# First cross attention of a decoder: scores from split q and k in one float32r pass, and five small operations on other engines

## What is computed

```
q = (x @ Wq + bq)                 # 16 heads of 8 channels
k = concat(fside @ Wk + bk, ctx)  # 248 keys: ctx itself serves as memory_k and memory_v
v = concat(fside @ Wv + bv, ctx)
attn = softmax((q @ k.T) * 8 ** -0.5, over keys)     # for each head
x = layernorm(x + (attn @ v) @ Wp + bp)
```

## Time and profile before

| | |
|---|---|
| median of 3 runs | 2702.93 us (2698.47 to 2707.09) |
| span of the profiled execution | 2695.8 us (its own time is not listed apart from the runs) |
| mean granted TensorE clock | 0.967 |
| TensorE busy, of the whole span | 2502.7 us (93%) |
| VectorE, ScalarE, GpSimd busy | 1849.6, 1737.7, 1401.1 us |
| DMA | 151.37 MB, mean 56 GB/s |

### The profile page before, as it was taken

The page is one execution under the profiler, slowest core; times in us unless marked ns, Lnnn a source line. Parts: engine busy times, 40 slices in busy tenths (PEclk is TensorE's granted clock), DMA queues, the critical chain, the costliest instruction groups (busy, mean ns, idle before and its releaser), DMA issues. The chain is left out here.

```text
span 2695.8 us, 95989 instructions
## 1 busy us (share of the span) xinstructions
PE 2502.7 (93%) x29950; PEld 2007.2 (74%) x29951; DVE 1849.6 (69%) x5434; ACT 1737.7 (64%) x6375; POOL 1401.1 (52%) x2914
## 2 busy tenths in 40 slices
PE   7999999799999999788889969999999799999995
PEld 6888888577777777487667758888888688888883
DVE  4565555588888888564334448888887388888886
ACT  4666666355555555213556638888888588888883
POOL 2333333233444344165774447777776266666664
PEclk9999999799999999899999979999999899999997
DMA  6332322211111111123332211111111111111100
GB/s 158 100 88 79 89 81 65 65 49 48 49 48 48 48 47 44 37 85 84 78 80 66 66 48 53 47 53 49 50 53 37 33 31 32 31 31 31 31 26 11
DMA packets 270161, 151.37 MB, mean 56 GB/s; under 512 B 51776, under 2 KB 263744, under 8 KB 270016
## 3 DMA queue, kind: packets, MB, share of 16 engines
q1 hardware_dynamic: 261312, 131.57, 18.2%
q0 software_dynamic: 8704, 17.97, 1.9%
HBM read 92.52 MB, written 48.51 MB: 52 GB/s over the span
## 5 line engine op out<-in xcount | busy, mean ns | idle before, releaser
L1187 ACT ACTIVATE pr<-psS,small 128x128 f32<-128x128 f32 x1024 | 366.7, 384 | 95.9 <-DVE small L1258 94.0
L1625 DVE TENSOR_REDUCE small<-psS 128x2 f32<-128x496 f32 x512 | 321.4, 669 | 90.3 <-PE psS L1489 89.1
L1577 ACT ACTIVATE pr<-psT 120x512 f32<-120x512 f32 (+1 forms) x384 | 215.1, 595 | 136.9 <-PE psT L1485 124.5
L1473 PE MATMUL psT<-cross_Qm,cross_xf 32*120 32x512 f32 (+1 forms) x768 | 292.1, 641 | 0.5 <-ACT pr L1577 0.2
L1187 ACT ACTIVATION_READ_ACCUMULATOR pr<-psS,small 128x1 f32 x1024 | 226.1, 221 | 0.0
L1478 PE MATMUL psS<-cross_xf,cross_Qm 32*128 32x248 f32 x1024 | 209.1, 428 | 1.1 <-DVE small L1625 1.1
L2172 POOL DMA_INDIRECT results<-experts_ob,experts_xb x144 | 138.5, 962 | 115.4 <-ACT experts_ob L1992 100.5
L1258 DVE TENSOR_REDUCE small<-psS 128x8 f32<-128x1024 f32 x128 | 156.7, 1224 | 60.5 <-PE psS L1152 60.3
L2112 DVE SCALAR_TENSOR_TENSOR experts_bgh<-experts_bth,psS 128x256 f32<-128x256 f32 x144 | 60.7, 421 | 198.9 <-ACT experts_bth L1984 198.9
L956 POOL TENSOR_SCALAR pr<-pr,small 128x120 f32<-128x120 f32 x512 | 180.4, 372 | 23.3 <-DVE small L910 23.3
L814 ACT ACTIVATE pr<-psS,small 128x120 f32<-128x120 f32 x512 | 179.0, 391 | 5.0 <-DVE small L929 5.0
(11 more groups left out here) (323 smaller groups left out, 8058.1 us busy)
## 6 DMA issues: line engine op xcount, KB each, us to landing
self_parts<-results SPq DMA_DIRECT2D x64, 192.0 KB, 2.4
slots<-blank SPq DMA_DIRECT2D x18, 520.0 KB, 4.5
experts_xb<-slots SPq DMA_DIRECT2D x144, 65.0 KB, 1.9
self_near<-in_x SPq DMA_DIRECT2D x128, 64.0 KB, 1.9
between<-self_xo SPq DMA_DIRECT2D x128, 64.0 KB, 1.6
cross_x<-between SPq DMA_DIRECT2D x128, 64.0 KB, 1.8
cross_res<-between SPq DMA_DIRECT2D x128, 64.0 KB, 1.8
self_x<-in_x SPq DMA_DIRECT2D x64, 64.0 KB, 1.8
```

The lines of the kernel that those rows point to most:

```text
L1187: last = act.activation(pr[e.slot % 4][:, cols], K.S[e.slot % 2][:, cols], ACT.Exp, bias=nmax[e.slot % 4][:, n:n + 1], accum_out=tot[k.slo ...
L1473: pe.matmul(to[0:size, :], xf[t.slot][rows(g), every][:, places[ck]], Qm[t.slot][rows(g), :], start=True, stop=False)
L1577: act.activation(PT[k][0:sizes[ck], 512 * n:512 * n + 512], T[turn[2 * r + n]][0:sizes[ck], :], ACT.Exp).then_inc(exped, 1)
L1625: dve.tensor_reduce(nmax[c.slot % 2][:, J * sg[n] + j0:J * sg[n] + j0 + 2], src, AX.X, ALU.max, negate=True).then_inc(maxed, 1)
```

## The change

- The products are `float32r` matmuls, one instruction each, over operands split into a high part (the value with its low 12 bits cleared) and a low part (the value less the high part). Head by head the 8 channels stand four times in the 32 rows of a row group: high and high, high and low, low and high, low and low parts of q and k. `Qm` and its mask are gone. The keys-major product of four heads becomes four products of 128 columns (`down`), the queries-major one stays 248 columns (`across`).
- q and k are projected one step earlier (for c+3 in place of c+2), with the columns of Wq, Wk and the biases in another order, made on the host. ScalarE writes them to `low`, SP loads the context's keys into the same tile, VectorE masks `low` into `high` (376 columns), GpSimd subtracts in place.
- The layout of the packs is made through DRAM: four stores (`high` and `low` whole; q's parts again; the keys' low part; the keys' high part) into `K.parts`, and one load of 128 x 1504 elements into `pack`. SP waits for GpSimd before the stores and for the landing of the four before the load.
- The cast of `NB`, the logits, xoT and oT go from VectorE to ScalarE, the last scaling (xo) from VectorE to GpSimd.
- Five constants of the first self attention are freed after it, to make room; for this the self attention's SP waits at its end until all blanks have landed.

The diff, cut to its core:

```diff
@@ attend_window, sync @@
                 sp.wait_ge(late_in, 16 * len(late))
+                sp.wait_ge(K.emptied, 16 * empty.shape[0])
@@ attend_keys_major @@
-        xf = [sb(f"xf{i}", [P, 2 * P + CTX + P]) for i in range(ring)]
-        qT = [sb(f"qT{i}", [P, P]) for i in range(2)]
-        Qm = [sb(f"Qm{i}", [P, J * P]) for i in range(ring)]
+        xf = [sb(f"xf{i}", [P, 2 * P]) for i in range(ring)]
+        part = [sb(f"part{i}", [P, 2, WIDE]) for i in range(2)]
+        high, low = ([v[:, i, :] for v in part] for i in range(2))
+        pack = [sb(f"pack{i}", [P, J, WIDE]) for i in range(ring)]
@@ sync @@
-                    a, l, s, o = c + 4, c + 3, c, c - 5
+                    a, l, s, o, h = c + 4, c + 3, c, c - 5, c + 2
...
+                        need(sp, v_ps, (a - 4).done())
+                        sp.dma_start(xf[a.slot][:, P:2 * P], D["t_fside"][a.n]).then_inc(f_in[a.slot], 16)
+                    if l.live:
+                        need(sp, parts_out[(l - 2).slot], (l - 2).p * STORES + STORES)
+                        sp.dma_start(low[l.slot % 2][:, 2 * P:], D["t_ctxq"][l.n]).then_inc(c_in[l.slot], 16)
...
-                    if l.live:
-                        need(sp, T_ps, (l - 4).done(2 * R, 4))
-                        sp.dma_start(xf[l.slot][:, P:2 * P], D["t_fside"][l.n]).then_inc(f_in[l.slot], 16)
-                        sp.dma_start(xf[l.slot][:, cT], D["t_ctx"][l.n]).then_inc(f_in[l.slot], 16)
+                    if h.live:
+                        need(sp, low_sb, h.done())
+                        to = K.parts[h.slot].rearrange("n p k -> p n k")
+                        mine = part[h.slot % 2]
+                        sp.dma_start(to[:, 0:4:3, :], mine[:]).then_inc(parts_out[h.slot], 16)
+                        sp.dma_start(to[:, 1:3, queries], mine[:, :, queries]).then_inc(parts_out[h.slot], 16)
+                        sp.dma_start(to[:, 1, keys], mine[:, 1, keys]).then_inc(parts_out[h.slot], 16)
+                        sp.dma_start(to[:, 2, keys], mine[:, 0, keys]).then_inc(parts_out[h.slot], 16)
+                        need(sp, T_ps, (h - 4).done(2 * R))
+                        need(sp, parts_out[h.slot], h.p * STORES + STORES)
+                        sp.dma_start(pack[h.slot][:].rearrange("p j k -> p (j k)"),
+                                     K.parts[h.slot].rearrange("n (s j) k -> s n (j k)", j=J)).then_inc(
+                            pack_in[h.slot], 16)
@@ tensor @@
-                        need(pe, masked, c.done())
-                        need(pe, qk_sb, c.done(2))
+                        need(pe, pack_in[c.slot], c.landed())
+
+                    def down(n, j):
+                        if t.live:
+                            g, to = tg[n], T[turn[2 * r + n]]
+                            pe.matmul(to[0:size, P * j:P * j + P], pack[t.slot][rows(g), j, places[ck]].bitcast(F32R),
+                                      pack[t.slot][rows(g), j, queries].bitcast(F32R), start=(j == 0), stop=False)
+
+                    def across(n, j):
+                        if c.live:
+                            g, to = sg[n], S[turn[2 * r + n]]
+                            last = pe.matmul(to[:, 256 * j:256 * j + CTX + P], pack[c.slot][rows(g), j0 + j, queries].bitcast(F32R),
+                                             pack[c.slot][rows(g), j0 + j, keys].bitcast(F32R), start=True, stop=True)
+                            if j == 1:
+                                last.then_inc(S_ps, 1)
...
+                        down(n, 0)
                         if c.live:
                             need(pe, maxed, (c if before[h] < h else c - 1).done(2 * R, before[h] + 1))
+                        across(n, 0)
+                    down(0, 1)
+                    down(1, 1)
+                    across(0, 1)
+                    down(0, 2)
+                    down(1, 2)
+                    across(1, 1)
+                    down(0, 3)
+                    down(1, 3)
@@ vector @@
+                    if h.live:
+                        need(dve, qk_sb, h.done(2))
+                        need(dve, c_in[h.slot], h.landed())
+                        need(dve, parts_out[c.slot], c.p * STORES + STORES)
+                        dve.tensor_scalar(high[h.slot % 2].bitcast(U32), low[h.slot % 2].bitcast(U32), UPPER, None,
+                                          ALU.bitwise_and).then_inc(top_sb, 1)
                     maxima(c, 0)
@@ gpsimd @@
-                        pool.tensor_tensor(Qm[b.slot][:].rearrange("p (j q) -> p j q", j=J),
...
+                    if h.live:
+                        need(pool, top_sb, h.done())
+                        pool.tensor_tensor(low[h.slot % 2], low[h.slot % 2], high[h.slot % 2],
+                                           ALU.subtract).then_inc(low_sb, 1)
```

More of the change, by code:

```diff
@@ L17 @@
 F32 = mybir.dt.float32
+F32R = mybir.dt.float32r
 BF16 = mybir.dt.bfloat16
@@ L173, in allocate @@
     K.tstep = K.sb("tstep", [P, 3])
+    K.alibi = K.sb("alibi", [P, WH * 48], F32, early)
+    K.Mself = K.sb("Mself", [P, WH * P], F32, early)
+    K.Nself = K.sb("Nself", [P, WH * P], F32, early)
+    K.Gram = K.sb("Gram", [P, 2 * P], F32, early)
+    K.blank = K.sb("blank", [P, BLANKS, ROW], F32, early)
 def set_up(K, D):
@@ L1335, in attend_keys_major @@
     sizes = (CTX, P)
-    places = (slice(0, CTX), slice(CTX, CTX + P))
+    WIDE = 2 * P + CTX
+    queries, keys = slice(0, P), slice(P, WIDE)
+    places = (slice(2 * P, WIDE), slice(P, 2 * P))
+    STORES = 4 * 16
     S = [K.SS[:, 512 * i:512 * i + 512] for i in range(3)]
@@ L1381, in attend_keys_major @@
         f_in = [sem(f"f_in{i}") for i in range(ring)]
+        c_in = [sem(f"c_in{i}") for i in range(ring)]
+        parts_out = [sem(f"parts_out{i}") for i in range(ring)]
+        pack_in = [sem(f"pack_in{i}") for i in range(ring)]
+        top_sb, low_sb, v_ps = sem("top_sb"), sem("low_sb"), sem("v_ps")
         xT_out = [sem(f"xT_out{i}") for i in range(ring)]
@@ L1389, in attend_keys_major @@
             "in_sb", "qk_sb", "v_sb", "nb_sb", "exped", "O_sb", "oT_sb"))
-        cleared, ready, masked, put_ctx, split, maxed = (sem(n) for n in (
-            "cleared", "ready", "masked", "put_ctx", "split", "maxed"))
+        cleared, ready, put_ctx, split, maxed = (sem(n) for n in (
+            "cleared", "ready", "put_ctx", "split", "maxed"))
         inverted, scaled = sem("inverted"), sem("scaled")
@@ L1553, in step @@
                         need(pe, in_sb, a.done())
-                        need(pe, f_in[a.slot], a.p * 32 + 32)
+                        need(pe, f_in[a.slot], a.landed())
                     if n.live:
@@ L1596, in step @@
-                        if (c - 5).live or (c - 6).live:
-                            need(act, turned_ps, (c - 5).done())
                         act.copy(xf[a.slot][:, 0:P], W0[:, 0:P]).then_inc(in_sb, 1)
+                    if n.live:
+                        need(act, y_ps, (n - 2).done())
+                        act.copy(oT[n.slot % 2][:], W0[:, 384:512]).then_inc(oT_sb, 1)
+                    if v.live:
+                        act.copy(routed.logits[:, bass.ds(v.n, 1), :].rearrange("p a e -> p (a e)"), W0[:, 256:256 + EXPERTS])
@@ L1599, in step @@
+                    if z.live:
+                        need(act, xT_out[z.slot], (z - 4).landed())
+                        act.copy(xoT[z.slot][:], W0[:, P:2 * P]).then_inc(turned_sb, 1)
                     exps(c, 2)
@@ L1647, in step @@
                     if b.live:
[L1648 to L1649 removed]
+                        need(dve, v_ps, b.done())
+                        if h.live:
+                            need(dve, qk_sb, h.done(2))
+                        elif w.live:
+                            need(dve, y_ps, w.done())
                         need(dve, O_ps, (b - 4).done(G))
@@ L1742, in step @@
                         pool.tensor_tensor(rs[w.slot % 2][:], ve[w.slot % 2][:], K.half[:, 0:1], ALU.pow).then_inc(lnroot, 1)
+                        need(pool, lnroot, w.done())
+                        need(pool, stored[w.slot], (w - 4).landed())
+                        need(pool, turned_ps, (w - 4).done())
                     if v.live:
```

116 lines of the change are left out of this document (43 added, 73 removed).

## The result

| | before | changed kernel |
|---|---|---|
| median of the timed runs | 2700.70 us (4 runs) | 2797.91 us (4 runs, 2789.34 to 2828.58) |
| ratio | | 1.038, 95% interval 1.034 to 1.042: slower |
| profiled execution, its span | span 2695.8 | 2806.37, span 2804.6 |
| mean granted clock of TensorE | 0.967 | 0.884 |
| first cross attention, first to last scores | 607.6 us | 704.0 us |

Executions that lie over 1.5% above the fastest one of the same kernel are left out of its ratio and interval.

A forecast was written before the change was run, and what follows sets the result against it. TensorE was taken to bound the first cross attention, with SP's loop the new bound after the change. 2702.9 - 607.6 + 63 x 9.2 (579.6) + 9.4 + 2 - 2 = 2684 us; range over the cases 2620 to 2745.

The forecast's parts named there:

- TensorE's part: First cross attention's score matmuls: one pass cuts a round from 1.28 to 0.86 us and TensorE's step to 7.8.
- The wait of 0.5 at the first maxima: TensorE at round 1 would wait some 0.5 us for VectorE's delayed first reduce, making compute's step about 8.3 us.
- the prediction's 0.8: How much longer, in us, TensorE's step would be if a load overlaps a running matmul only in another row group.
- The small operations: Work moved among VectorE, ScalarE and GpSimd: about 6.6, 6.9 and 4.0 us a step, none passing TensorE's 7.8.
- SP's queue: Twelve issues a step and the wait for four stores (4.7 us) make SP's loop 9.2 us, the new bound.
- Ends of the stage: First scores 9.4 us later, first load of the cross attention +2, last steps -2.
- the sum, 63 x 9.2: 63 steps of the first cross attention at 9.2 us, 579.6 in all, replacing the 607.6 measured before.
- the list of what would prove the forecast wrong: Profile signs: SP waiting for low_sb, store hole over 4 us, slow or doubled matmuls, first maxima holding TensorE over 1 us.
- The rivals: Compute is the bound (0.2, 2628 us), stores land late (0.2, 2754), one pass not cheaper (0.1, 2702 to 2714).
- late stores: Rival: stores to the packs land after 5.8 us, SP's loop is 10.3 and the time 2754 us; chance 0.2.
- The slower outcome: Chance 0.3 that the kernel gets slower: 0.06 from the main forecast, 0.2 from stores landing late, 0.04 from one pass not cheaper.
- rival B: Set up for the experiments, not the prediction: one-pass score matmuls let the clock fall by themselves; no chance given.

The follow-up runs named there:

- warm: Changed kernel plus 12 bf16 filler matmuls of 128 columns ahead of TensorE's wait for the pack: 2797.53 us, ratio 0.9935 to the kernel before on the same chip.
- actload: Changed kernel with ScalarE, not SP, issuing the pack's load behind the step before's first exponentials: 2650.04 us, ratio 0.974 to the kernel before (four of seven runs).
- f32_slowsp: Changed kernel with plain f32 scores on the same packs and four more 64 KB loads a step on SP: 2804.97 us, one execution; kernel before 2699.99.
- early: actload_warm plus 96 more fillers before the first step's wait for its pack: 2767.65 us, ratio 0.984 to the kernel before.
- actload_warm: Changed kernel with ScalarE issuing the pack's load and 12 fillers a step ahead of TensorE's wait for the pack: 2631.37 us, ratio 0.974 to the kernel before.

## Why the prediction was wrong, step by step

- **TensorE's part** was right at the clock it was priced for: one pass streams like bf16 (266 ns at least for 248 columns, where one plain f32 instruction has 367), a round lasts 0.83 us (976.23 to 977.06) for 0.86, and the step 7.83 for 7.8. The wait of 0.5 at the first maxima is not there. That two loads of one row group follow at 0.11 held, against the Trainium skill's rule ("TensorE: Matmul & The Clock Gate", what overlaps and what doesn't), which would have put the step at 8.6 by the prediction's 0.8.
- **The small operations** were off one by one and none mattered: mask 0.35 for 0.45, subtraction 0.99 for 0.8, xo 0.80 on GpSimd for 0.4, the NB cast 0.59 on ScalarE for 0.69.
- **SP's queue**: a loop of 8.68 in one step and 9.08 over 33 (warm) for 9.2. The wait for the stores is 4.1 for 4.7, the issues around it 4.6 for 4.5. (The prediction calls the stores' rows 1504 and 992 bytes; those of the 128 KB store, q's parts again, are 512.)
- **Ends of the stage**: first scores 10.6 us later for 11.4, but by luck in the parts: the cross attention's first load moved by 5.1 us (477.84 to 482.93) for 2, and the way from there to the first scores grew by 5.5 for 9.4.
- **The step that failed is the sum, 63 x 9.2.** It priced all steps at the granted clock of 1.00 read from rows 1, where TensorE was busy in every microsecond. The change brings waits of TensorE at the pack, behind which the clock falls, and one-pass scores, with which it can stay down; 33 steps took 13.4 us for 9.2, all or most of each at 0.50. No rival had it, and the list of what would prove the forecast wrong did not name the clock. With the clock held by fillers the measured ratio is 0.9935, the forecast's 0.9930. A smaller lack of the same term: 63 x 9.2 has no slow start, while the 607.6 that it replaces has one, and `warm` took 586.3 for 579.6.
- **The rivals**: the stores landed early, not late, and compute did bound the step at full clock in `actload`. The slower outcome had a chance of 0.3, but mostly by a mechanism (late stores) that the runs rule out.

The Trainium skill ("TensorE: Matmul & The Clock Gate", HAM oscillation) describes bursts of matmuls with waits for a DMA between them, at which the clock falls to half; by the same page (what's actually happening) activity gives it back. The fall at 585 us agrees, behind a wait of 1.27 us for the pack, and so do the returns after 3 to 14 us in the stage of f32_slowsp and of the kernels with fillers, early's start apart. Two things differ, and there the measurement decides: in actload the clock fell with no wait of TensorE for a DMA near, behind 0.46 us at a cast, and with one-pass scores it did not recover in 270 us in which TensorE was busy without a gap.

**What stays open.** No run had one-pass scores with no idle at all and no fillers; the nearest are stretches of some 90 and 107 us in actload, at full clock, so rival B is unlikely as a cause of the falls but not excluded (the fall in `early`). Whether it is the one-pass kind of the score matmuls or the smaller amount of work that they make in the array, with their loads between, that keeps the clock down, no run tells, since none changed one without the other. Nor is it known why one wait brings the clock down and a longer one does not, or what ends a long stretch at 0.50. f32_slowsp, on which the comparison with plain f32 rests, is one execution.

## What to carry to other kernels

A full TensorE row says nothing of its speed: read the granted clock beside it, before for what the sum rests on, and after before any other row. When an edit makes TensorE's work lighter or gives it gaps, price the steps at both levels of the clock, and try a few cheap filler matmuls ahead of the wait. A clock that falls is half of the matter: look also at how long it stays down. A move of small operations that is worth nothing while another engine binds can be worth 0.3 us of a step of 8.3 and keep the clock up besides, once that bound is gone, so judge it after the large part, not before.

## What the runs showed of the hardware that was not expected

- TensorE stayed at half clock for 270 us with 240.00 of 240 us busy, and a step went from 7.83 to 13.59, by 1.74 and not by 2.
- The clock fell behind waits of TensorE of 0.4 to 2.4 us, with one-pass and with plain f32 scores. It was back after 3 or 7 us with plain f32 scores, and down for up to 290 us with one-pass scores and no fillers.
- 12 bf16 filler matmuls a step made a kernel 4.3% faster (by two ratios, from two chips).
- When ScalarE issues the load, the same stores land later: the 376 KB store after 4.4 us for 2.7 (actload_warm against the change), with the pack's load of 752 KB under way beside it, by the likeliest reading; TensorE did not wait for the pack.
- A scaling of 128 columns with two operations takes 799 ns on GpSimd and 337 on VectorE.
